# A fused attention and gated projection kernel on Trainium2: the output projection's eight tiles of a chunk issued in one run at the chunk's end instead of two runs of four, and one exponential moved ahead of a sigmoid

## The chip, the cores and the metric

One Trainium2 chip, all 8 cores, one program on each; every core computes one batch element. The metric is the device time in microseconds of the slowest core. Each core runs its engines (PE matmul, DVE vector, ACT scalar, POOL and SP, which here issue DMAs) from instruction streams of their own, joined by semaphores.

## What is computed

Per batch element there are 2048 tokens of width 4096. The reference, cut to what matters:

```python
xn = layernorm(x)
q, k, v = xn @ Wq, xn @ Wk, xn @ Wv            # 32 q heads, 8 k/v heads of 128
o_lin = gla_scan(softmax(q), softmax(k), v, log_sigmoid(k) / 16)   # recurrent state S per head
y = sliding_window_attn(rope(q), rope(k), v)    # window 64
s = bf16(0.5 * y + 0.5 * o_lin) @ Wo            # output projection
g = silu(xn @ W0.T + b0 + masked low-rank terms)
out = x + s * g
```

## The kernel before, in words

The work runs in stages. Stage 1 normalises x and transposes it into `bigA`. Stage 2 computes g (4096 base matmuls, line 210) and spills it to `g_sp` in HBM. Stage 3 computes v, k and q (lines 272, 299, 326) and spills them. Then the attention goes over 16 chunks of 128 tokens, `for c in range(NCH)` at line 464, and the output projection, called p5 in the code, is woven into it.

A chunk has three parts. The **k part** loads `kin` (line 467), takes sigmoid and log of it on ACT (lines 474 and 476), scans it on DVE (line 478), takes exponentials (482, 485, 490), and `ek`, the exponential of `kin` (line 492), whose column sums are two PE matmuls `denk` (495, 496); ACT turns them into reciprocals `rk` (499 to 502). The **q part** goes over 8 groups of four q heads: `eq` (555), `denq` (558), `p4rq` (562, 563), rotary products (569, 577 to 583). The **score part** goes over the same 8 groups: scores (602 to 614), exponentials (620, 624), sums (628, 631), reciprocals (638, 639), products (642, 646), the linear term (650, 655), and, two groups later, `emit_pass2` with the output matmuls (417 to 422), the copy into `bigA` (435), the state update (442, 452, 459). In this program chunks c=0 to 3 are attention alone; from c=4 on each chunk also carries 8 tiles of the projection for the 512 tokens finished four chunks and more ago; 32 tiles for the last 512 tokens follow after c=15.

A **p5 tile** is emitted by `emit_p5_jtile` (line 358). It is 32 matmuls into the one PSUM tile `pWo` (line 381), a copy by ACT, `scop` (390), a multiply with g on DVE, `sg` (393), a DMA transpose issued from ACT's queue, `sgt` (397), an add of x on DVE, `xadd` (402), and the store of the result from SP's queue, `outst` (406). The tile's g comes by `gld` from SP's queue (367), its x by `xld` from POOL's queue (371). Two tiles share one block of Wo, 2 MB in HBM, loaded from POOL's queue by `emit_p5_block` (352) into one of two buffers, so that four tiles can have their weights in SBUF at once. A matmul group of a tile waits for the copy of the tile before.

Every queue takes its instructions in the order of the program, and a wait holds all that is behind it. On SP's queue the order is gld of tile n, outst of tile n, gld of tile n+1; outst of n waits for xadd of n, so gld of n+1 is not issued before xadd of n. On POOL's queue a Wo block stands behind the xld of the tile before it, and that xld waits for the xadd two tiles back. On DVE, sg and xadd of a tile stand ahead of whatever the program has next, and on ACT the transpose of a tile stands ahead of what is next there.

Of the 8 tiles of a chunk, before, four stand between the q part and the score part, and four after the score part, ahead of two small copies on DVE, `sbf` (668) and `p4odone` (670); the next chunk's `vin` load (470) waits for `p4odone`. SP's queue has nothing of the score part in it, nor has POOL's.

Of the kernel before, what the change touches and what calls it, by code (L numbers as in the profile page):

```python
# [9 lines left out]
AF = mybir.ActivationFunctionType  # L10
# [22 lines left out]
class Walk:  # L33
# [26 lines left out]
    def op(self, stream, name, emit_fn, waits=()):  # L60
        serial = stream in ("V", "S", "G")
        sem = STREAM_SEM[stream]
        if self.mode == "collect":
            self._wait(waits)
            return
        if self.mode == "count":
            if serial:
                self.C[sem] += 1
                if name is not None:
                    self.evt[name] = (sem, self.C[sem])  # L70
            elif name is not None and name in self.waited:
                self.C[sem] += 1
                self.evt[name] = (sem, self.C[sem])
            return
        if self.stream != stream:
            return
        self._wait(waits)
        if serial and self.C[sem] > 0:
            self.eng.wait_ge(self.sems[sem], self.C[sem])
        instr = emit_fn(self.eng)  # L80
        if serial:
            self.C[sem] += 1
            instr.then_inc(self.sems[sem], 1)
        elif name is not None and name in self.waited:
            self.C[sem] += 1
            instr.then_inc(self.sems[sem], 1)
# [34 lines left out]
def build_walk(w, t):  # L121
    op, dma = w.op, w.dma
# [9 lines left out]
    for i in range(NTT):  # L132
# [5 lines left out]
            waits=[f"p1xn.{i-2}"] if i >= 2 else [])  # L138
# [3 lines left out]
           waits=[f"p1x.{i}"] + ([f"p1r.{i-2}"] if i >= 2 else []))  # L142
# [3 lines left out]
           waits=[f"p1x.{i}"] + ([f"p1xn.{i-2}"] if i >= 2 else []))  # L146
# [6 lines left out]
           waits=[f"p1sq.{i}"])  # L153
# [4 lines left out]
           waits=[f"p1r.{i}", f"p1nm.{i}"] + ([f"p1tr.{i-2}"] if i >= 2 else []))  # L158
# [4 lines left out]
            waits=[f"p1xn.{i}"])  # L163
# [5 lines left out]
        waits=P1_END)  # L169
    dma("G", "w_bt", lambda e: e.dma_start(out=t["bt"], in_=t["bt_h"][:]), waits=P1_END)  # L170
    xn = t["bigA"][:].rearrange("p (k tt) -> p k tt", k=32)
    for ts in range(4):
        def mm_h(e, ts=ts):
# [6 lines left out]
           waits=["w_acat", f"p1tr.{NTT-1}"] + ([f"p2hev.{ts-1}"] if ts else []))  # L180
        op("S", f"p2hev.{ts}",
           lambda e, ts=ts: e.copy(t["h"][:, ts * 512:(ts + 1) * 512], pb[0][:]),
           waits=[f"p2h.{ts}"])
# [9 lines left out]
    for lt in range(128):  # L193
        j, ts = lt // 4, lt % 4
# [4 lines left out]
            waits=P1_END if lt < 2 else [f"p2tl3.{lt - 2}"])  # L199
# [60 lines left out]
    for vq in range(4):  # L260
# [4 lines left out]
            waits=[f"p2mm.{119 + 8 * vq}"] if vq < 2 else [f"p3vmm.{(vq-1)*16 - 1}"])  # L265
        for tt in range(16):
            it = vq * 16 + tt

            def mm_v(e, vq=vq, tt=tt, it=it):
# [6 lines left out]
               waits=[f"wv.{vq}"] + ([f"p3vev.{it-2}"] if it >= 2 else [f"p2sil.{126}", f"p2sil.{127}"]))  # L276
            op("S", f"p3vev.{it}",
               lambda e, it=it: e.copy(t["ev"][it % 4][:, 0:256], pb[4 + it % 2][:, 0:256]),
               waits=[f"p3vmm.{it}"] + ([f"p3vsp.{it-4}"] if it >= 4 else P2_POOL_FREE),)
# [4 lines left out]
                waits=[f"p3vev.{it}"])  # L284
    for b in range(4):
# [4 lines left out]
            waits=[f"p3vmm.{47 + 16 * b}"] if b < 2 else [f"p3kmm.{(b-1)*8 - 1}"])  # L290
        for sub in range(8):
            j2, ts = sub // 4, sub % 4
            j = b * 2 + j2
            it = b * 8 + sub

            def mm_k(e, b=b, j2=j2, ts=ts, it=it):
# [7 lines left out]
               waits=[f"wk.{b}"] + ([f"p3kev.{it-2}"] if it >= 2 else [f"p3vev.{62 + it}"]))  # L304
            op("S", f"p3kev.{it}",
               lambda e, it=it: e.copy(t["ev"][it % 4], pb[4 + it % 2][:]),
               waits=[f"p3kmm.{it}"] + ([f"p3ksp.{it-4}"] if it >= 4 else [f"p3vsp.{60 + it}"]))
# [4 lines left out]
                waits=[f"p3kev.{it}"])  # L312
    for b in range(16):
# [3 lines left out]
            waits=[f"p3kmm.{23 + 8 * b}"] if b < 2 else [f"p3qmm.{(b-1)*8 - 1}"])  # L317
        for sub in range(8):
            j2, ts = sub // 4, sub % 4
            j = b * 2 + j2  # L320
            it = b * 8 + sub

            def mm_q(e, b=b, j2=j2, ts=ts, it=it):
# [7 lines left out]
               waits=[f"wqb.{b}"] + ([f"p3qev.{it-2}"] if it >= 2 else [f"p3kev.{30 + it}"]))  # L331
            op("S", f"p3qev.{it}",
               lambda e, it=it: e.copy(t["ev"][it % 4], pb[4 + it % 2][:]),  # L333
               waits=[f"p3qmm.{it}"] + ([f"p3qsp.{it-4}"] if it >= 4 else [f"p3ksp.{28 + it}"]))
# [4 lines left out]
                waits=[f"p3qev.{it}"])  # L339
# [5 lines left out]
       waits=P3_SPILLED + [f"p3qev.{127}"])  # L345
# [11 lines left out]
    def emit_p5_jtile(ts, j):  # L357
        b, j2 = j // 2, j % 2
        it = j * 4 + ts
        if j2 == 0:  # L360
            emit_p5_block(ts, b)
        ei = len(p5_seq)
        prev = p5_seq[-1] if p5_seq else None
        pprev = p5_seq[-2] if len(p5_seq) >= 2 else None
        p5_seq.append(it)
        dma("SY", f"gld.{it}",
            lambda e, j=j, ts=ts, ei=ei: e.dma_start(
                out=t["gld5"][ei % 2], in_=t["g_sp"][j, :, ts * 512:(ts + 1) * 512]),
            waits=[f"p2gs.{it}"] + ([f"sg.{pprev}"] if pprev is not None else []))
        dma("G", f"xld.{it}",  # L370
            lambda e, j=j, ts=ts, ei=ei: e.dma_start(  # L371
                out=t["xld5"][ei % 2],
                in_=bass.AP(t["x_h"].tensor, ts * 512 * D + j * 128,
                            [[D, 128], [128 * D, 4], [1, 128]])),
            waits=[f"xadd.{pprev}"] if pprev is not None else [])

        def mm_s(e, b=b, j2=j2, ts=ts):
            wb = t["wobuf"][b % 2].rearrange("p (k m) -> p k m", k=32)
            off = (4 * ts % 8) * 128
            for k in range(32):  # L380
                ii = e.matmul(t["pWo"][:], wb[:, k, j2 * 128:j2 * 128 + 128],  # L381
                              bass.AP(t["bigA"][:].tensor, k * 1024 + off,
                                      [[32 * NT, 128], [1, 512]]),
                              start=(k == 0), stop=(k == 31))
            return ii
        op("T", f"p5mm.{it}", mm_s,
           waits=[f"wo.{ts}.{b}", f"oev.{4*ts+3}.{KVH-1}"] +
                 ([f"scop.{prev}"] if prev is not None else []))
        op("S", f"scop.{it}",
           lambda e, ei=ei: e.copy(t["sgf5"][ei % 2], t["pWo"][:]),  # L390
           waits=[f"p5mm.{it}"] + ([f"sg.{pprev}", f"outst.{pprev}"] if pprev is not None else []))
        op("V", f"sg.{it}",
           lambda e, it=it, ei=ei: e.tensor_tensor(t["sgv5"][ei % 2], t["sgf5"][ei % 2],  # L393
                                                   t["gld5"][ei % 2], ALU.mult),
           waits=[f"scop.{it}", f"gld.{it}"] + ([f"sgt.{pprev}"] if pprev is not None else []))
        dma("S", f"sgt.{it}",
            lambda e, it=it, ei=ei: e.dma_start_transpose(
                t["sgt5"][ei % 2].rearrange("p (r q) -> p r q", r=4),
                t["sgv5"][ei % 2]),
            waits=[f"sg.{it}"] + ([f"xadd.{pprev}"] if pprev is not None else []))  # L400
        op("V", f"xadd.{it}",
           lambda e, ei=ei: e.tensor_tensor(t["sgf5"][ei % 2].bitcast(BF16).bitcast(F32),  # L402
                                            t["xld5"][ei % 2], t["sgt5"][ei % 2], ALU.add),
           waits=[f"sgt.{it}", f"xld.{it}"] + ([f"outst.{pprev}"] if pprev is not None else []))
        dma("SY", f"outst.{it}",
            lambda e, j=j, ts=ts, ei=ei: e.dma_start(
                out=bass.AP(t["out_h"].tensor, ts * 512 * D + j * 128,
                            [[D, 128], [128 * D, 4], [1, 128]]),
                in_=t["sgf5"][ei % 2].bitcast(BF16).bitcast(F32)),
            waits=[f"xadd.{it}"])  # L410
# [53 lines left out]
    for c in range(NCH):  # L464
        cr = c % 2
        dma("SY", f"kin.{c}",
            lambda e, c=c: e.dma_start(out=t["kin"], in_=t["k_sp"][c, :, :]),
            waits=P3_SPILLED + ([f"p4kdone.{c-1}"] if c else []))
        dma("SY", f"vin.{c}",
            lambda e, c=c, cr=cr: e.dma_start(out=t["vring"][cr], in_=t["v_sp"][c, :, :]),  # L470
            waits=(P3_SPILLED + ["s_zero"] if c < 2 else []) +
                  ([f"p4odone.{c-1}"] if c >= 1 else []) +
                  ([f"sadd.{c-2}.{KVH-1}"] if c >= 2 else []))
        op("S", f"sig.{c}", lambda e: e.activation(t["ksig"], t["kin"], AF.Sigmoid),
           waits=[f"kin.{c}"])
        op("S", f"lsig.{c}", lambda e: e.activation(t["ksig"], t["ksig"], AF.Ln), waits=[])  # L476
# [4 lines left out]
           waits=[f"lsig.{c}", "c_onesf"])  # L481
# [7 lines left out]
           waits=[f"lam.{c}"] + ([f"sdec.{c-1}.{KVH-1}"] if c else []))  # L489
        op("S", f"expli.{c}", lambda e: e.activation(t["expli"], t["lam"], AF.Exp, scale=-INV16),  # L490
           waits=[f"lam.{c}"])
        op("S", f"ek.{c}", lambda e: e.activation(t["ekt"], t["kin"], AF.Exp),  # L492
           waits=[f"kin.{c}"])
        op("T", f"denk.{c}",
           lambda e: (e.matmul(pb[4][:], t["ones_sb"][:], t["ekt"][:, 0:512], start=True, stop=True),  # L495
                      e.matmul(pb[5][:], t["ones_sb"][:], t["ekt"][:, 512:1024], start=True, stop=True))[-1],
# [86 lines left out]
                   lambda e, g=g: e.tensor_tensor(t["sqa8"][g], t["sq2"], t["sq3"], ALU.add)],  # L583
               waits=[f"rotq.{c}.{g}"])

        if c >= 4:
            _ts = (c - 4) // 4
            _j0 = 8 * ((c - 4) % 4)
            for _j in range(_j0, _j0 + 4):
                emit_p5_jtile(_ts, _j)  # L590
        for g in range(KVH):
            gr = g % 2
            hs = slice(g * 128, (g + 1) * 128)
# [66 lines left out]
                emit_pass2(c, g - 2, cr)  # L660
        emit_pass2(c, KVH - 2, cr)
        emit_pass2(c, KVH - 1, cr)
        if c >= 4:
            _ts = (c - 4) // 4
            _j0 = 8 * ((c - 4) % 4)
            for _j in range(_j0 + 4, _j0 + 8):
                emit_p5_jtile(_ts, _j)
        op("V", f"sbf.{c}", lambda e: e.tensor_copy(t["Sbf"], t["S"]),
           waits=[f"sadd.{c}.{KVH-1}"])
        op("V", f"p4odone.{c}", lambda e: e.tensor_copy(t["qt2"][:, 0:1], t["qtil3"][0][:, 0:1]),  # L670
           waits=[f"oev.{c}.{KVH-1}", f"oev.{c}.{KVH-2}"])

    for j in range(32):
        emit_p5_jtile(3, j)
    P4_END = [f"p4odone.{NCH-1}", f"sadd.{NCH-1}.{KVH-1}", f"sbf.{NCH-1}",
# [267 lines left out]
```

## Time and profile before

| | |
|---|---|
| median of 2 runs | 6549.73 us |
| lowest and highest | 6541.64 and 6557.82 us |
| the profiled execution's own time | 6541.64 us |
| its span (slowest core, core 4) | 6540.1 us |
| spans of the 8 cores | 6479.1 to 6540.1 us |
| busy: PE, DVE, ACT, POOL | 4181.4, 1384.1, 1244.0, 372.7 us |

The profile is of the slowest core. Busy times are summed over the whole span and say little on a single stage, since the stages have different limits. The chunks c=4 to 14 take 2239 us of the span, and c=15 with the last 32 tiles about 640.

### The profile page before, as it was taken

Reading aid. Unit: us, or ns where it says so; the run is one execution under the profiler, and the core shown is the slowest. Engines: PE = TensorE matmul, PEld = TensorE weight load, DVE = VectorE, ACT = ScalarE, POOL = GpSimd, SP = SyncE. Lnnn points to the kernel's source line nnn. Section 1 sums busy time; section 2 is a strip of 40 time slices with the busy share of each in tenths; the row PEclk is TensorE's granted clock in tenths of the full one; section 3 lists DMA queues with packets and bytes.
Section 4 is the critical chain, followed back from the end, with each engine's and each line's share of the span. In section 5 each row is a group of like instructions: output and inputs, shape, how many; then the busy total and the mean of one; then the engine's idle time right before and its main releaser. Section 6 shows DMA issues by size and latency. Waiting matters only on the chain.

```text
span 6540.1 us, 54373 instructions; the slowest of 8 cores (6479.1 to 6540.1 us)
## 1 busy us (share of the span) xinstructions
PE 4181.4 (64%) x18464; PEld 1753.7 (27%) x18464; DVE 1384.1 (21%) x2344; ACT 1244.0 (19%) x1790; POOL 372.7 (6%) x368
## 2 busy tenths in 40 slices
PE   0047777787799999999844545545456444564555
PEld 0012332232258444444310112211122111121222
DVE  2212222222220000000044332322322323223111
ACT  4420000000001000000144332222322223223000
POOL 0000000000000000000000000000000000000111
PEclk9998988898899999999955667767677676776888
DMA  5454334434443333333310246364554544544898
GB/s 144 137 100 92 85 91 93 93 80 94 90 88 58 58 58 58 58 58 58 57 23 17 37 82 100 61 100 79 86 100 72 90 89 75 100 78 84 120 148 136
DMA packets 821746, 544.02 MB, mean 83 GB/s; under 512 B 241248, under 2 KB 757600, under 8 KB 819296
## 3 DMA queue, kind: packets, MB, share of 16 engines
q0 software_dynamic: 460576, 320.89, 32.1%
q1 hardware_dynamic: 225216, 186.09, 10.9%
q10 hardware_dynamic: 135680, 33.57, 3.2%
q8 instruction: 150, 2.46, 0.2%
q14 instruction: 124, 1.02, 0.1%
HBM read 634.83 MB, written 92.27 MB: 111 GB/s over the span
## 4 chain that ended last, share of the span: by engine, by line
PE 46%; DMA 24%; ACT 12%; DVE 9%; issue 5%; ACTq 3%; SPq 1%; DVEq 1%; POOLq 0%; POOL 0%
PE pb L326 14%; PE pb L210 13%; DMA bigA<-bigA 9%; DMA bigA<-g_sp 8%; DMA pool<-maskt 4%; PE pb L272 3%; PE pb L299 3%; PE pWo L381 3%; ACTq L160 2%; PE pb L239 2%; DMA pool<-q_sp 2%; DVE bigA L393 1%; DVE bigA L402 1%; ACT pool L245 1%; ACT pool L140 1%
## 5 line engine op out<-in xcount | busy, mean ns | idle before, releaser
L381 PE MATMUL pWo<-bigA 128*128 128x512 bf16 x4096 | 960.7, 395 | 258.3 <-DMA bigA<-wo 176.6
L210 PE MATMUL pb<-bigA,pool 128*128 128x512 bf16 x4096 | 935.3, 388 | 134.2 <-ACT pool L245 133.3
L326 PE MATMUL pb<-bigA,pool 128*128 128x512 bf16 x4096 | 884.2, 379 | 0.0
L381 PEld LDWEIGHTS pWo<-bigA 128*128 128x128 bf16 x4096 | 407.4, 101 | 806.4 <-issue 384.2
L227 DVE TENSOR_TENSOR pool<-pb,pool 128x512 bf16<-128x512 f32 x512 | 354.2, 692 | 1180.8 <-PE pb L239 695.8
L210 PEld LDWEIGHTS pb<-bigA,pool 128*128 128x128 bf16 x4096 | 399.0, 99 | 676.0 <-issue 240.0
L326 PEld LDWEIGHTS pb<-bigA,pool 128*128 128x128 bf16 x4096 | 400.8, 98 | 483.3
L478 DVE TENSOR_TENSOR_SCAN pool<-onesf_sb,pool 128x128 f32<-128x128 f32 x128 | 54.4, 425 | 1455.5 <-ACT pool L476 1444.0
L245 ACT ACTIVATE pool<-pb,b_sb 128x512 f32<-128x512 f32 x128 | 87.9, 687 | 1366.2 <-PE pb L239 1366.2
L558 PE MATMUL pb<-pool,twos_sb 128*128 128x512 bf16 x128 | 74.9, 585 | 381.5 <-ACT pool L555 381.5
L495 PE MATMUL pb<-pool,ones_sb 128*128 128x512 bf16 x16 | 9.3, 584 | 456.2 <-ACT pool L492 456.2
L176 PE MATMUL pb<-bigA,pool 128*128 128x512 bf16 x128 | 30.6, 400 | 409.5 <-DMA pool<-acat 406.8
L390 ACT COPY bigA<-pWo 128x512 f32<-128x512 f32 x128 | 74.9, 585 | 1125.3 <-PE pWo L381 1054.6
L628 PE MATMUL pb<-pool,twos_sb 128*128 128x512 bf16 x128 | 63.7, 498 | 326.3 <-ACT pool L624 317.0
L371 POOL DMA_DIRECT2D bigA<-x x128 | 96.6, 755 | 3065.0 <-DVE bigA L402 2930.4
L393 DVE TENSOR_TENSOR bigA<-bigA 128x512 bf16<-128x512 f32 x128 | 88.6, 692 | 739.2 <-DMA bigA<-g_sp 602.0
L333 ACT CAST pool<-pb 128x512 bf16<-128x512 f32 x128 | 74.9, 585 | 809.2 <-PE pb L326 809.2
L272 PE MATMUL pb<-pool,bigA 128*128 128x256 bf16 x2048 | 225.9, 274 | 1.0 <-ACT pool L245 1.0
L299 PE MATMUL pb<-bigA,pool 128*128 128x512 bf16 x1024 | 221.2, 379 | 0.0
L402 DVE TENSOR_TENSOR bigA<-bigA 128x512 f32<-128x512 f32 x128 | 88.6, 692 | 617.9 <-DMA bigA<-bigA 617.9
L272 PEld LDWEIGHTS pb<-pool,bigA 128*128 128x128 bf16 x2048 | 201.3, 98 | 26.2 <-issue 1.9
L219 PE MATMUL pb<-pool 16*128 16x512 bf16 x512 | 53.6, 408 | 215.9 <-DVE pool L227 215.9
(112 smaller groups left out, 3423.2 us busy)
## 6 DMA issues: line engine op xcount, KB each, us to landing
bigA<-wo POOLq DMA_DIRECT2D x64, 2048.0 KB, 17.4
pool<-maskt POOLq DMA_DIRECT2D x128, 512.0 KB, 4.6
pool<-x SPq DMA_DIRECT2D x16, 2048.0 KB, 8.3
pool<-w0t POOLq DMA_DIRECT2D x16, 2048.0 KB, 18.1
g_sp<-pool SPq DMA_DIRECT2D x128, 256.0 KB, 2.7
pool<-wq POOLq DMA_DIRECT2D x16, 2048.0 KB, 17.2
bigA<-x POOLq DMA_DIRECT2D x128, 256.0 KB, 5.2
bigA<-g_sp SPq DMA_DIRECT2D x128, 256.0 KB, 4.5
```

What stands on the lines that cost most here:

```text
L160: lambda e, i=i, ib=ib: e.dma_start_transpose(t["bigA"][:].rearrange("p (c tt) -> p c tt", c=32)[:, :, i * 128:(i + 1) * 128], t["xn_tm"][ ...
L210: ii = e.matmul(pb[bk][:], wb[:, k, j2 * 128:j2 * 128 + 128], xn[:, k, ts * 512:(ts + 1) * 512], start=(k == 0), stop=False)
L227: lambda e, l=l, ts=ts, it=it: e.tensor_tensor(t["tl"][l], pb[l][:], t["mbig"][it % 2].rearrange("p (l4 tt) -> p l4 tt", l4=4)[:, l, :], A ...
L239: ii = e.matmul(pb[bk][:], t["id128_sb"][:], t["tl"][l], start=False, stop=(l == 3))
L245: lambda e, it=it, j=j, bk=bk: e.activation(t["gv"][it % 2], pb[bk][:], AF.Silu, bias=t["b0_sb"][:, j:j + 1]),
L272: ii = e.matmul(pb[4 + it % 2][:, 0:256], xn[:, k, tt * 128:(tt + 1) * 128], wb[:, k, :], start=(k == 0), stop=(k == 31))
L299: ii = e.matmul(pb[4 + it % 2][:], wb[:, k, j2 * 128:j2 * 128 + 128], xn[:, k, ts * 512:(ts + 1) * 512], start=(k == 0), stop=(k == 31))
L326: ii = e.matmul(pb[4 + it % 2][:], wb[:, k, j2 * 128:j2 * 128 + 128], xn[:, k, ts * 512:(ts + 1) * 512], start=(k == 0), stop=(k == 31))
L371: lambda e, j=j, ts=ts, ei=ei: e.dma_start(out=t["xld5"][ei % 2], in_=bass.AP(t["x_h"].tensor, ts * 512 * D + j * 128, [[D, 128], [128 * D ...
L381: ii = e.matmul(t["pWo"][:], wb[:, k, j2 * 128:j2 * 128 + 128], bass.AP(t["bigA"][:].tensor, k * 1024 + off, [[32 * NT, 128], [1, 512]]), ...
L393: lambda e, it=it, ei=ei: e.tensor_tensor(t["sgv5"][ei % 2], t["sgf5"][ei % 2], t["gld5"][ei % 2], ALU.mult),
L402: lambda e, ei=ei: e.tensor_tensor(t["sgf5"][ei % 2].bitcast(BF16).bitcast(F32), t["xld5"][ei % 2], t["sgt5"][ei % 2], ALU.add),
```

## The change

Two edits. The p5 tiles of a chunk are emitted in one run of eight, after the score part and after `sbf` and `p4odone`, and no longer in two runs of four. And `ek` is emitted as the first ACT operation of the k part, ahead of the sigmoid, with one more wait, for `sk` of the chunk before on DVE, which reads the buffer that `ek` writes.

```diff
@@ -471,6 +471,8 @@
+        op("S", f"ek.{c}", lambda e: e.activation(t["ekt"], t["kin"], AF.Exp),
+           waits=[f"kin.{c}"] + ([f"sk.{c-1}"] if c else []))
         op("S", f"sig.{c}", lambda e: e.activation(t["ksig"], t["kin"], AF.Sigmoid),
            waits=[f"kin.{c}"])
@@ -489,8 +491,6 @@
-        op("S", f"ek.{c}", lambda e: e.activation(t["ekt"], t["kin"], AF.Exp),
-           waits=[f"kin.{c}"])
         op("T", f"denk.{c}",
@@ -583,11 +583,6 @@
-        if c >= 4:
-            _ts = (c - 4) // 4
-            _j0 = 8 * ((c - 4) % 4)
-            for _j in range(_j0, _j0 + 4):
-                emit_p5_jtile(_ts, _j)
         for g in range(KVH):
@@ -660,16 +655,15 @@
-        if c >= 4:
-            _ts = (c - 4) // 4
-            _j0 = 8 * ((c - 4) % 4)
-            for _j in range(_j0 + 4, _j0 + 8):
-                emit_p5_jtile(_ts, _j)
         op("V", f"sbf.{c}", lambda e: e.tensor_copy(t["Sbf"], t["S"]),
            waits=[f"sadd.{c}.{KVH-1}"])
         op("V", f"p4odone.{c}", lambda e: e.tensor_copy(t["qt2"][:, 0:1], t["qtil3"][0][:, 0:1]),
            waits=[f"oev.{c}.{KVH-1}", f"oev.{c}.{KVH-2}"])
-
+        if c >= 4:
+            ts = (c - 4) // 4
+            j0 = 8 * ((c - 4) % 4)
+            for j in range(j0, j0 + 8):
+                emit_p5_jtile(ts, j)
```

On PE, in chunk c=4 of the kernel before, the first four tiles (128 matmuls, L381) stand between the last rotary matmul of the q part (L569) and the first scores (L602):

```order
L558 MATMUL pb<-pool,twos_sb 128x512
L569 MATMUL pb<-pool,rmat_sb 128x512
L381 MATMUL pWo<-bigA 128x512 x128
L602 MATMUL pb<-bigA,pool 128x512
L603 MATMUL pb<-i4rep_sb,mcur_sb 128x512
```

On PE in the same chunk of the changed kernel the scores (its L597 is the L602 of before) follow the q part directly:

```order
L569 MATMUL pb<-pool,rmat_sb 128x512
L558 MATMUL pb<-pool,twos_sb 128x512
L569 MATMUL pb<-pool,rmat_sb 128x512
L597 MATMUL pb<-bigA,pool 128x512
L598 MATMUL pb<-i4rep_sb,mcur_sb 128x512
```

The four tiles have left this place. At the chunk's end of the changed kernel all 256 matmuls of the eight tiles stand in a row, between the last state matmul (L442) and the next chunk's denk (L495):

```order
L422 MATMUL pb<-pool 128x512
L442 MATMUL pS<-pool 128x128
L381 MATMUL pWo<-bigA 128x512 x256
L495 MATMUL pb<-pool,ones_sb 128x512
L496 MATMUL pb<-pool,ones_sb 128x512
```

On ACT in the k part of chunk c=4, before: sigmoid (L474), log (L476), the three exponentials of the scan (L482, L485, L490), ek (L492), then the first operation on denk's result (L499):

```order
L474 ACTIVATE pool<-pool 128x1024
L476 ACTIVATE pool<-pool 128x1024
L482 ACTIVATE pool<-pool 128x1024
L485 ACTIVATE st<-pool 128x8
L490 ACTIVATE pool<-pool 128x1024
L492 ACTIVATE pool<-pool 128x1024
L499 ACTIVATE pool<-pb 128x512
```

On ACT in the changed kernel, where L474 is ek, L476 the sigmoid, L478 the log and L484, L487, L492 the three exponentials of the scan:

```order
L474 ACTIVATE pool<-pool 128x1024
L476 ACTIVATE pool<-pool 128x1024
L478 ACTIVATE pool<-pool 128x1024
L484 ACTIVATE pool<-pool 128x1024
L487 ACTIVATE st<-pool 128x8
L492 ACTIVATE pool<-pool 128x1024
L499 ACTIVATE pool<-pb 128x512
```

Nothing now stands on ACT between the last scan exponential and L499. On SP's and POOL's queues the order of the DMAs is the same in both kernels.

## Rows read from the trace of the kernel before

**Rows 1.** Page, section 2: 40 slices of 163.5 us each.

```profile
PE   0047777787799999999844545545456444564555
PEclk9998988898899999999955667767677676776888
DMA  5454334434443333333310246364554544544898
```

**Rows 2.** Timeline of ACT: k parts of chunks 4 and 15 begin (start us, us).

```profile
3661.82 1.06 ACT L474 ACTIVATE pool<-pool 128x1024 f32<-128x1024 bf16 x1
...
5900.99 1.06 ACT L474 ACTIVATE pool<-pool 128x1024 f32<-128x1024 bf16 x1
```

**Rows 3.** Windows: chunk 11 by stage (length, busy and count by engine, PEclk, DMA, GB/s).

```profile
5088.30:5143.60 55.30, 10.92 (x29) 2.86 (x30) 22.24 (x43) 23.93 (x35) 0.00 (x0) 0.50 0.40 63
5143.60:5195.00 51.40, 30.98 (x135) 13.04 (x133) 7.94 (x14) 4.68 (x8) 3.98 (x4) 0.83 0.62 97
5195.00:5238.60 43.60, 32.53 (x92) 7.74 (x92) 21.25 (x41) 19.74 (x34) 2.44 (x2) 0.73 0.45 67
5238.60:5286.50 47.90, 29.62 (x129) 12.55 (x128) 6.88 (x10) 3.95 (x8) 3.95 (x4) 0.86 0.59 104
5286.50:5291.50 5.00, 0.00 (x0) 0.00 (x0) 0.88 (x3) 1.29 (x2) 2.44 (x2) 0.50 0.72 219
```

**Rows 4.** Windows: chunk 3, which has no tiles; its score part.

```profile
3607.40:3658.40 51.00, 41.08 (x97) 8.99 (x96) 23.71 (x46) 21.91 (x38) 0.00 (x0) 0.58 0.00 1
```

**Rows 5.** Chain that ended last, core 4, from the fifth tile of chunk 15 on.

```profile
6073.73 0.70 DVE bigA L402
6075.04 5.10 DMA bigA<-g_sp
6080.30 0.70 DVE bigA L393
6081.12 11.61 DMA bigA<-bigA
6093.03 0.70 DVE bigA L402
```

**Rows 6.** Timeline, PE and POOL, core 4: the run from chunk 15's fifth tile on.

```profile
6052.94 7.07 PE L381 MATMUL pWo<-bigA 128*128 128x512 bf16 x32
...
6075.78 1.71 POOL L352 DMA_DIRECT2D bigA<-wo  x1
...
6101.80 8.60 PE L381 MATMUL pWo<-bigA 128*128 128x512 bf16 x32 [17.80 <-DMA bigA<-wo]
```

**Rows 7.** Timeline of DVE, core 4: xadd of the run's eighth and 32nd tile.

```profile
6168.40 0.69 DVE L402 TENSOR_TENSOR bigA<-bigA 128x512 f32<-128x512 f32 x1 [2.88 <-DMA bigA<-bigA]
...
6492.92 0.69 DVE L402 TENSOR_TENSOR bigA<-bigA 128x512 f32<-128x512 f32 x1 [3.24 <-DMA bigA<-bigA]
```

**Rows 8.** Timeline of core 7: the same run's first tile and eighth xadd.

```profile
5978.41 7.07 PE L381 MATMUL pWo<-bigA 128*128 128x512 bf16 x32
...
6082.90 0.69 DVE L402 TENSOR_TENSOR bigA<-bigA 128x512 f32<-128x512 f32 x1 [2.89 <-DMA bigA<-bigA]
```

**Rows 9.** Timeline of core 1: the same two.

```profile
6030.25 7.07 PE L381 MATMUL pWo<-bigA 128*128 128x512 bf16 x32
...
6153.20 0.69 DVE L402 TENSOR_TENSOR bigA<-bigA 128x512 f32<-128x512 f32 x1 [2.91 <-DMA bigA<-bigA]
```

**Rows 10.** Timeline of ACT: the k part of chunk 12.

```profile
5290.20 1.28 ACT L474 ACT_TABLE_LOAD   x1 [18.39 <-DMA pool<-k_sp]
...
5292.62 1.28 ACT L476 ACT_TABLE_LOAD   x1
...
5299.41 1.06 ACT L482 ACTIVATE pool<-pool 128x1024 bf16<-128x1024 f32 x1 [4.44 <-DVE pool L478]
...
5302.02 1.06 ACT L492 ACTIVATE pool<-pool 128x1024 bf16<-128x1024 bf16 x1
5304.38 0.60 ACT L499 ACTIVATE pool<-pb 128x512 f32<-128x512 f32 x1 [1.31 <-PE pb L496]
```

## The prediction

> **What bounds the kernel now.** I read the 40 slices of the page first, then the starts of the chunks, then the stages of one chunk, and last the chain of waits through the projection's tiles.
>
> The slices [rows 1] show two kinds of time. In the first half PE is busy seven to nine tenths; from about 3300 us on it is busy four to six tenths, at a granted clock of 0.6 to 0.7. The change touches that second part alone. Its size comes from the starts of the k parts [rows 2]: chunks 4 to 14 take 5900.99 - 3661.82 = 2239.2 us, or 203.6 us each, eleven times. Chunk 11 is close to that mean, and the windows cut it at the borders of its parts [rows 3]: 55.3 us for the k and q parts, 51.4 for the first run of four tiles (first matmul to last xadd on DVE), 43.6 for what is left of the score part, 47.9 for the second run, and 5.0 until the next chunk's first ACT operation, together 203.2.
>
> In no part is one engine full. In a run of four PE is busy 30 of 48 to 51 us [rows 3]. The chain shows why [rows 5]: it goes from an xadd on DVE to the next g (gld, 5.1 us), the multiply sg (0.7), the DMA transpose (11.6) and the next xadd, in a ring, with no matmul in it. By the order of SP's queue gld of a tile is not issued before xadd of the tile before, so the ring is serial. A tile on PE takes 7.07 us, and the next starts 8.0 after it; the ring took 6093.03 - 6073.73 = 19.3 us that time, with a Wo load of 2 MB issued at 6075.78 in flight [rows 5, 6]. So a run of tiles is paced by DMAs and DVE's place in the ring, and PE runs ahead until the weights are missing.
>
> **Part 1, the two runs become one.** Removed from the middle of the chunk: a run that occupies 51.4 us. But the score part then no longer finds its head start. Before, PE had issued the first scores while DVE was still at its xadds, and found a warmer clock (0.73). Without tiles ahead of it the same score part took 51.0 us in chunk 3, at 0.58 [rows 4]. I take 50.0; the bounds are 43.6 and 51.0. The gld, xld and transposes of those four tiles leave too, and go where the matmuls go.
>
> Added at the end: a run of eight in place of one of four, 47.9 us before. What does it take? The trace has it: in chunk 15 the second run of four goes straight on into the 32 last tiles, so 36 stand in a row, with the same two buffers for Wo, and the first four tiles' weights already there, as they will be in the changed kernel. From the run's first matmul to the end of its eighth xadd it took
>
> - core 4: 6168.40 + 0.69 - 6052.94 = 116.2 us [rows 6, 7]
> - core 7: 6082.90 + 0.69 - 5978.41 = 105.2 us [rows 8], the shortest of the eight cores
> - core 1: 6153.20 + 0.69 - 6030.25 = 123.6 us [rows 9], the longest; the middle of the eight is about 109.
>
> It is not twice 47.9 = 95.8, since only four tiles have their weights beforehand. The Wo block of tiles 5 and 6 is issued on POOL's queue behind an xld that waits for the second tile's xadd: 6075.78, 22.8 us into the run, and tile 5 starts at 6101.80 after PE stood 17.8 us for it [rows 6]. The next two blocks follow in the same way and slow the transposes of the tiles whose ring they cross. Before, of a chunk's four blocks two landed beside the k, q or score part, where nothing waited for them: by the order of POOL's queue one was issued behind the last xld of each run. Afterwards it is one of four. Further on in the long run a pair of tiles costs (6492.92 - 6168.40) / 12 = 27.0 us [rows 7], which would make 47.9 + 2 x 27.0 = 102.0 for eight. I take 108: between 102.0 and core 4's own 116.2, near the middle of the eight cores. The bounds are 95.8 and 123.6.
>
> On the last wait: `p4odone` now stands ahead of the tiles, so that `vin` is free earlier. I cost it at nothing, because SP's queue keeps `kin` and `vin` behind the eighth outst in any case, which waits for the eighth xadd. The 5.0 us from there to the sigmoid stay [rows 3]. Nor does the first part of the chunk gain from the move: POOL and SP issue in the same order as before.
>
> **Part 2, ek moved.** Before, from ek's start to the start of the reciprocals on ACT 5304.38 - 5302.02 = 2.36 us pass: ek itself, and a wait of 1.31 for PE [rows 10]. Now denk is done under the sigmoid and the scan, and these 2.36 go. At the front ek costs its 1.06 and the step to the next, 1.1 together, since sigmoid, log and DVE's scan follow one on another. Net -1.2 us per chunk; bounds -2.4 (if the front were hidden) and +0.1 (if a table load of 1.28 were added each time). The added wait on sk of the chunk before is met in the k part of that chunk, a whole q and score part earlier, and holds nothing behind it.
>
> No table load should be added past the first chunk: L482's exponential runs after L476's log without one [rows 10], so both are in one table, and that is the one resident when the next chunk's ek comes, since only copies, scalings, exponentials and logs lie between. In chunk 0 one is added, +1.3.
>
> The Trainium skill, page "ScalarE: Activation LUTs", section "Table sets: the hidden batching unit", asks for calls to be grouped by table, and putting an exponential ahead of a sigmoid looks like the opposite. The same page ("What ACT_TABLE_LOAD costs") gives 2.66 us for a switch with its drain, 43 us over 16 chunks if each had one more; the trace has 1.28 us for a load, and the next operation on its heels, which would make 21.
>
> **The sum.** A chunk from 4 to 14: 55.3 - 1.2 + 50.0 + 108 + 5.0 = 217.1, against 203.6: +13.5, times 11 = +148.5. Chunk 15 and the end: before, its long run starts 6052.94 - 5900.99 = 152.0 us after its sigmoid; afterwards at 55.3 - 1.2 + 50.0 = 104.1, 47.9 earlier, but with four tiles more in it, 2 x 27.0 = 54.0: +6.1. Chunks 0 to 3: 4 x -1.2 + 1.3 = -3.5. Together +151. The profiled execution's own time was 6541.64 (span 6540.1), 8 us under the median of 6549.73; against the median the forecast is 6549.7 + 151 = 6701 us, 2.3% slower. About 2%, 131 us, is what a measurement of this kernel can tell from no change.
>
> **The rivals.**
>
> *Paced by PE (faster).* If the second four tiles came at PE's own step of 8.0 us, a run of eight would be 47.9 + 32 = 79.9, a chunk 189.0, and the whole 11 x -14.6 + 2.6 = -158: 6392 us. It decides from the point where ring and weights of a tile take under 8.0 us. For it: one start-up and one tail fewer per chunk, and a run holds the clock at 0.83 to 0.86, where the parts around it have 0.50 and 0.73 [rows 3]. Against it: eight of eight cores took 105 us or more.
> The Trainium skill says it as a rule: page "Perfetto Trace Analysis", section "Matmul Optimizations", asks that matmuls execute back to back in batches, because the engine scales with its use. By that rule the time would be this rival's. The fifth tile, which takes 8.60 us after its wait and not 7.07 [rows 6], speaks against it: the longer batch has the wait inside.
>
> *The second four cost a run of their own (no change).* With 95.8 for eight and 51.0 for the score part a chunk takes 205.9, +2.3, and with the other terms (+3.6) the whole +29: 6579 us. With the 102.0 of the long run's pace and 50.0 it is 211.1, +7.5, together +85: 6635. For it: in chunk 15 all cores come to load Wo without a pause, in the middle of the kernel a core does so half of the time. Against it: core 7, with little in its way, still took 105.2.
>
> *Contention as in core 4 or worse (slower still).* With 116.2 the whole is +151 + 11 x 8.2 = +241: 6791 us; with core 1's 123.6 it is 6872. For it: the measured time is that of the slowest core, and this one is core 4 here. Against it: it would have to be so in every chunk.
>
> *The change does not do what it says.* The ek edit could be lost behind DVE's scan: 15 to 20 us at most, within the range.
>
> **How the numbers follow.** A run of eight near 108 (104 to 114): 0.55, of which most lies over +131. Cheaper runs, no change: 0.27. Contention at 114 or more: 0.13. Paced by PE: 0.05. Slower by over 2% is then 0.48 + 0.13 = 0.61, within 2% 0.07 + 0.27 = 0.34, faster 0.05. The range is 6600 to 6795: the lower end is between the two figures of the no-change rival, the upper one core 4's run in every chunk.
>
> **What would show it.** The starts of the k parts 215 to 219 us apart in chunks 5 to 14. In each run of eight two waits of PE for a DMA into bigA from wo, 8 to 18 us each, at its fifth and seventh tile; 104 to 114 us from first matmul to eighth xadd. The score part at 47 to 51 us with a granted clock near 0.6. In the k part one table load ahead of the sigmoid and one ahead of the log, and no wait of ACT for L496. A spacing under 200 us would prove the forecast wrong, and a run of eight under 100 us would name the step.

## The result, and the profile after

The change makes the kernel slower, by less than 2% but beyond doubt: ratio to the kernel before 1.0139, 95% interval 1.0123 to 1.0155. Its executions take 6634.7 to 6647.0 us, against 6541.0 to 6557.8 before; by the ratio it is 91 us more than the 6549.7. The profiled execution took 6638.9 us. (Either kernel has executions in which one die runs at a lower clock, some 260 to 420 us longer; ratios and times leave these out, and where an experiment's profile shows such a die, its means below are of the four cores at the usual clock, which are named.)

The page of the changed kernel, sections 1 and 2 in part, and the tile group of section 5 (busy and mean, idle before, releaser), then the same group of the kernel before:

```profile
span 6637.3 us, 54375 instructions; the slowest of 8 cores (6569.7 to 6637.3 us)
PE 4258.5 (64%) x18464; PEld 1763.2 (27%) x18464; DVE 1384.0 (21%) x2344; ACT 1245.9 (19%) x1791; POOL 372.6 (6%) x368
...
DMA  5454434443443333333200247633674446633998
...
L381 PE MATMUL pWo<-bigA 128*128 128x512 bf16 x4096 | 994.5, 405 | 537.7 <-DMA bigA<-wo 467.1
```

```profile
L381 PE MATMUL pWo<-bigA 128*128 128x512 bf16 x4096 | 960.7, 395 | 258.3 <-DMA bigA<-wo 176.6
```

PE's time ahead of the tiles' matmuls rose to 537.7 us, 467.1 of it on loads of Wo. The kernel before had 258.3 and 176.6. The DMA digits of the chunks now swing between 3 and 7, where [rows 1] had mostly 4 and 5.

The stages of chunk 11 on core 5, the slowest here: k and q parts, score part, run of eight, and what follows to the next chunk (columns as in [rows 3]):

```profile
5165.20:5218.20 53.00, 11.10 (x28) 2.72 (x28) 22.33 (x44) 25.39 (x36) 0.00 (x0) 0.50 0.40 72
5218.20:5265.70 47.50, 36.83 (x97) 8.44 (x97) 23.58 (x45) 21.92 (x38) 0.00 (x0) 0.66 0.00 1
5265.70:5368.80 103.10, 60.56 (x258) 25.43 (x257) 13.27 (x20) 6.29 (x12) 10.38 (x10) 0.84 0.80 125
5368.80:5372.50 3.70, 0.00 (x0) 0.00 (x0) 0.04 (x1) 0.00 (x0) 2.44 (x2) 0.50 0.69 170
```

During the score part the DMA engines now do nothing (share 0.00), and during the run they are 0.80 busy; before, both runs and the score part between them had 0.45 to 0.62 [rows 3].

Mean over the eight cores and chunks 4 to 14, in us:

| | before | after |
|---|---|---|
| from the k part's first operation to the end of the q part | 55.5 | 54.0 |
| first run of four | 48.7 | none |
| score part, or what is left of it after that run | 44.4 | 49.0 |
| last run (four, or eight) | 48.6 | 103.8 |
| to the next chunk's first operation | 5.3 | 4.4 |
| chunk | 202.2 | 211.2 |

The column of before adds up to 0.3 too much, mostly because the run's first matmul starts 0.2 before the last rotary product ends. So the eight tiles themselves cost 103.8 - 97.3 = 6.5 more and the score part 4.6 more; 1.5 come back in the k and q parts and 0.9 in the step to the next chunk: +9.0 a chunk, 99 us in 11 chunks.

The run of eight of chunk 11, core 5: xadd of the second to the last tile (DVE), the Wo loads (POOL) and the two matmul groups that wait (PE), from the timelines of these engines:

```profile
5286.83 0.69 DVE L402 TENSOR_TENSOR bigA<-bigA 128x512 f32<-128x512 f32 x1 [2.92 <-DMA bigA<-bigA]
5305.70 0.69 DVE L402 TENSOR_TENSOR bigA<-bigA 128x512 f32<-128x512 f32 x1 [9.20 <-DMA bigA<-bigA]
5315.22 0.69 DVE L402 TENSOR_TENSOR bigA<-bigA 128x512 f32<-128x512 f32 x1 [2.90 <-DMA bigA<-bigA]
5334.93 0.69 DVE L402 TENSOR_TENSOR bigA<-bigA 128x512 f32<-128x512 f32 x1 [8.67 <-DMA bigA<-bigA]
5343.97 0.69 DVE L402 TENSOR_TENSOR bigA<-bigA 128x512 f32<-128x512 f32 x1 [2.90 <-DMA bigA<-bigA]
5358.12 0.69 DVE L402 TENSOR_TENSOR bigA<-bigA 128x512 f32<-128x512 f32 x1 [8.18 <-DMA bigA<-bigA]
5368.14 0.69 DVE L402 TENSOR_TENSOR bigA<-bigA 128x512 f32<-128x512 f32 x1 [2.91 <-DMA bigA<-bigA]
...
5288.88 1.72 POOL L352 DMA_DIRECT2D bigA<-wo  x1
5317.34 1.69 POOL L352 DMA_DIRECT2D bigA<-wo  x1
5346.01 1.71 POOL L352 DMA_DIRECT2D bigA<-wo  x1
...
5310.40 9.37 PE L381 MATMUL pWo<-bigA 128*128 128x512 bf16 x32 [13.71 <-DMA bigA<-wo]
5338.95 8.75 PE L381 MATMUL pWo<-bigA 128*128 128x512 bf16 x32 [11.18 <-DMA bigA<-wo]
```

The spacing of the xadds alternates: 18.9, 9.5, 19.7, 9.0, 14.2, 10.0. The wait in brackets alternates with it: a transpose lands 2.9 us after DVE's last work when no load is in flight, and 8.2 to 9.2 us after it when a load of Wo was issued some 2 us after the xadd before. I call such a step of the ring a turn.

The kernel before has one such long turn in each run of four, the third. Here are the second and third xadd and the load that was issued between them, in the second run of chunk 10, core 5:

```profile
5012.20 0.69 DVE L402 TENSOR_TENSOR bigA<-bigA 128x512 f32<-128x512 f32 x1 [2.92 <-DMA bigA<-bigA]
5026.56 0.69 DVE L402 TENSOR_TENSOR bigA<-bigA 128x512 f32<-128x512 f32 x1 [8.29 <-DMA bigA<-bigA]
...
5014.25 1.71 POOL L352 DMA_DIRECT2D bigA<-wo  x1
```

Over all cores of the changed kernel, 408 of the tiles' 1024 transposes had a load of Wo of their own core in flight at some time between issue and landing: they took 8.4 us (median). The other 616 took 2.5. In the last 32 tiles, where every core has a load of Wo in flight about two thirds of the time, none of the 120 with a load of their own core beside them took under 7.2 us, and none of the 136 without one over 3.3. So it is the core's own load that counts, and not those of the other cores.

The k part of chunk 12, ACT, core 5:

```profile
5372.55 1.06 ACT L474 ACTIVATE pool<-pool 128x1024 bf16<-128x1024 bf16 x1 [16.05 <-DMA pool<-k_sp]
5373.68 1.28 ACT L476 ACT_TABLE_LOAD   x1
...
5376.10 1.28 ACT L478 ACT_TABLE_LOAD   x1
...
5384.35 1.06 ACT L492 ACTIVATE pool<-pool 128x1024 bf16<-128x1024 f32 x1
5385.49 0.60 ACT L499 ACTIVATE pool<-pb 128x512 f32<-128x512 f32 x1
```

ek (L474) runs without a table load, two loads follow as before, and L499 comes on the heels of L492, where [rows 10] had ek and a wait of 1.31 between.

### The profile page after: what moved, and what is told of

It is laid out like the page before. It is cut to its first block, busy times and chain, and to the rows that moved or that the text cites. A ratio compares the mean times of both kernels' runs of the same rounds, so it can differ in the third digit from the quotient of the medians.

```text
span 6637.3 us, 54375 instructions; the slowest of 8 cores (6569.7 to 6637.3 us)
## 1 busy us (share of the span) xinstructions
PE 4258.5 (64%) x18464; PEld 1763.2 (27%) x18464; DVE 1384.0 (21%) x2344; ACT 1245.9 (19%) x1791; POOL 372.6 (6%) x368
## 3 DMA queue, kind: packets, MB, share of 16 engines
q1 hardware_dynamic: 225216, 186.09, 10.6%
## 4 chain that ended last, share of the span: by engine, by line
PE 45%; DMA 25%; ACT 12%; DVE 9%; issue 5%; ACTq 3%; SPq 1%; DVEq 1%; POOLq 0%; POOL 0%
PE pb L326 13%; PE pb L210 13%; DMA bigA<-bigA 9%; DMA bigA<-g_sp 9%; DMA pool<-maskt 4%; PE pb L272 3%; PE pb L299 3%; ACTq L160 2%; PE pb L239 2%; PE pWo L381 2%; DMA pool<-q_sp 1%; DVE bigA L393 1%; DVE bigA L402 1%; ACT pool L245 1%; ACT pool L619 1%
## 5 line engine op out<-in xcount | busy, mean ns | idle before, releaser
L381 PE MATMUL pWo<-bigA 128*128 128x512 bf16 x4096 | 994.5, 405 | 537.7 <-DMA bigA<-wo 467.1
L381 PEld LDWEIGHTS pWo<-bigA 128*128 128x128 bf16 x4096 | 413.2, 103 | 1113.8 <-issue 712.1
L495 PE MATMUL pb<-pool,ones_sb 128*128 128x512 bf16 x16 | 9.4, 585 | 243.1 <-ACT pool L474 243.1
```

## The experiments

I went in with two theories for the length of a run. R: it is a serial ring of gld, sg, transpose and xadd, and a Wo load in flight stretches a turn. W: it is PE's wait for weights inside the run, most of the 467 us of the page.

**The two edits apart.** `e1_run8_only` is the changed kernel with ek at its old place:

```diff
-        op("S", f"ek.{c}", ...)                 # ahead of sig.{c}
+        op("S", f"ek.{c}", ...)                 # after expli.{c}, as before
```

> The eight tiles in one run at the chunk's end, ek left where it was. Theory R (a run is paced by the serial ring gld, sg, transpose, xadd, and a Wo load in flight makes every second turn of it long): a run of eight stays at 101 to 107 us, the chunk is 1.0 to 1.3 us longer than in the changed kernel, 211.2 + 1.2 = 212.4 us, and the whole is 15 to 20 us over the changed kernel, 1.016 to 1.018 of before. Rival (ek ahead of the sigmoid delays the scan and costs time): the whole is under the changed kernel, below 1.0139.

Measured: 1.0217 of before, interval 1.0093 to 1.0341. The interval is too wide to part the two expectations; the trace does it. On cores 4 to 7 the chunk is 212.2 us and the run of eight 103.9. The chunk is 1.4 longer than on the same cores of the changed kernel (210.8), and that is the step from the last xadd to the next chunk's first operation, 5.8 us for 4.3. All the loss sits in the order of the tiles.

`e2_ek_only` is the kernel before with ek moved:

> The kernel before with ek moved ahead of the sigmoid and nothing else. If the step saves 1.2 us in each of 16 chunks and costs one table load of 1.3 in the first: 18 us less, 0.997 of before, and no wait of ACT for denk's second matmul. If the front of the k part were hidden too: 2.4 us a chunk, 0.994. If it costs: over 1.000.

Measured: 0.9952, interval 0.9908 to 0.9995. The chunk falls from 202.2 to 200.9, 1.3 us, as the first expectation has it, and the step from the last xadd to the next chunk's first operation from 5.3 to 3.9 (18 us, 0.997, is inside the interval; 0.994 cannot be excluded by the ratio, but a chunk shorter by 2.4 would be at 199.8). The edit is a small gain.

**Ring or weights.** `e7_run8_wo_ahead` issues each load one tile earlier:

```diff
-        if j2 == 0:
-            emit_p5_block(ts, b)
+        if ei == 0:
+            emit_p5_block(ts, b)
...
+        if j2 == 1 and ei < 127:
+            emit_p5_block(ts if b < 15 else ts + 1, (b + 1) % 16)
         dma("G", f"xld.{it}",
```

> The changed kernel with each Wo block issued on POOL one tile earlier, ahead of the xld of the odd tile before it. Theory R: PE's two waits in a run fall from about 12 us each to 2 to 5, but the ring goes on as before, a run of eight 100 to 106 us, the whole within 30 us of the changed kernel. Theory W: each of the two waits falls by about 8 us and the run with them, to 88 us; chunks at 195, the whole about 200 us under the changed kernel.

Measured: 1.0226, interval 1.0097 to 1.0355; chunk 219.7, run of eight 112.4. Both theories missed: W by sign, since the waits for weights are gone (see the tile group of the page below, where PE's idle time is put down to ACT's copy) and the run is 8.6 us longer; R by size.

```profile
L383 PE MATMUL pWo<-bigA 128*128 128x512 bf16 x4015 | 997.3, 408 | 475.8 <-ACT bigA L392 470.8
```

The timelines of chunk 11, core 5, show what I had not thought of (xadds of the first, second, third, seventh and eighth tile, then the loads, then the fifth tile's matmuls):

```profile
5306.56 0.69 DVE L404 TENSOR_TENSOR bigA<-bigA 128x512 f32<-128x512 f32 x1 [3.35 <-DMA bigA<-bigA]
5320.63 0.69 DVE L404 TENSOR_TENSOR bigA<-bigA 128x512 f32<-128x512 f32 x1 [8.15 <-DMA bigA<-bigA]
5332.39 0.69 DVE L404 TENSOR_TENSOR bigA<-bigA 128x512 f32<-128x512 f32 x1 [2.93 <-DMA bigA<-bigA]
...
5387.47 0.69 DVE L404 TENSOR_TENSOR bigA<-bigA 128x512 f32<-128x512 f32 x1 [2.93 <-DMA bigA<-bigA]
5403.02 0.69 DVE L404 TENSOR_TENSOR bigA<-bigA 128x512 f32<-128x512 f32 x1 [8.64 <-DMA bigA<-bigA]
...
5310.35 1.70 POOL L352 DMA_DIRECT2D bigA<-wo  x1 [1.73 <-PE pWo L383]
5334.44 1.71 POOL L352 DMA_DIRECT2D bigA<-wo  x1
5363.71 1.69 POOL L352 DMA_DIRECT2D bigA<-wo  x1
5389.52 1.72 POOL L352 DMA_DIRECT2D bigA<-wo  x1
...
5331.72 8.78 PE L383 MATMUL pWo<-bigA 128*128 128x512 bf16 x32 [6.29 <-ACT bigA L392]
```

The fifth tile now waits for ACT's copy, and so for the ring. The long turns are the second, fourth, sixth and eighth: the fourth load, which in the changed kernel was issued after the eighth xadd, now falls into the run. That gave theory C: a turn is about 10 us alone and 16 with a load in flight, and what counts is how many loads cross a run (cross means: are in flight during it).

`e5_run8_gld_ahead` opens the ring at gld:

```diff
+        if ei + 1 < 128:
+            emit_gld(ei + 1)      # gld of the next tile, ahead of
         dma("SY", f"outst.{it}",  # this tile's store
```

> The changed kernel with gld of tile n+1 issued on SP ahead of outst of tile n, so that the ring is broken at gld; the Wo loads stay as they are. Theory R (the ring is the pace): short turns go from 9 to 8 us (PE's step), long ones from 19 to 13 or so, a run of eight from 104 to 84 to 92 us, chunks from 211 to 193 to 199, the whole 200 to 330 us under the changed kernel. Theory W (the pace is the Wo loads, for which PE waits at the fifth and seventh tile): a run of eight stays at 98 to 104 and the whole within 60 us of the changed kernel.

Measured: 6529.6 us in a single execution, too few for a ratio; the chunk on cores 4 to 7 is 204.4, the run of eight 97.2, where these cores had 210.8 and 102.9. That lies between the two expectations, and both missed: R by size, with 5.7 us of the 12 to 20, and W because the run is just under its 98 to 104 and a chunk 6.4 shorter, 70 us in 11. Three rows of core 5, chunk 11 (the fourth and fifth xadd and the fifth tile's matmuls), show why:

```profile
5212.78 0.69 DVE L412 TENSOR_TENSOR bigA<-bigA 128x512 f32<-128x512 f32 x1 [8.22 <-DMA bigA<-bigA]
5230.00 0.69 DVE L412 TENSOR_TENSOR bigA<-bigA 128x512 f32<-128x512 f32 x1 [9.55 <-DMA bigA<-bigA]
...
5209.96 8.78 PE L391 MATMUL pWo<-bigA 128*128 128x512 bf16 x32 [9.37 <-DMA bigA<-wo]
```

With the ring open it meets the loads at once: the transposes take 8 to 9 us also in turns that were short, and the fifth tile's turn starts from its late weights. In the means of these cores the waits for the transpose are 8.7 to 9.6 us in five of the eight turns. Both limits lie close together; neither theory alone was the whole.

**Taking the loads away.** `e3_run8_no_wo` and `e4_run4_no_wo` leave out all Wo loads but the first two, in the changed kernel and in the one before:

```diff
+        if ts == 0 and b < 2:
             dma("G", f"wo.{ts}.{b}", ...)
...
-           waits=[f"wo.{ts}.{b}", ...
+           waits=[f"wo.0.{b % 2}", ...
```

> The changed kernel without the Wo loads after the first two blocks (the tiles then use wrong weights; 124 MB of loads are left out). Theory C (a run is a serial ring of about 9 us a tile, and what makes it longer is each Wo load that is in flight during it): a run of eight falls from 104 to 13 + 7 x 9.1 = 77 us or a little under, the last 32 tiles from 27 to 18 us a pair, PE waits for ACT or DVE only. Rival P (with the weights there, PE's own step of 8.0 us is the pace): 8.0 us a tile, 70 us a run and 16.0 us a pair.

> The kernel before without the Wo loads after the first two blocks (wrong weights for the tiles, the loads left out). Theory C: a run of four falls from 48.6 to 13 + 3 x 9.1 = 40 us; two runs of four then take 80 and one of eight 77, so that the two orders of the tiles come to within 1% of each other in the whole, the chunk of this kernel at 184 to 188 us. Rival (two short runs lose more than one long one in start and end, loads apart): this kernel is over 2% slower than the changed one without its loads.

Measured: 6220.9 us with runs of eight, 6197.4 with runs of four, 0.4% apart, from one execution each. The spans of the eight cores have the same mean, 6171.5 and 6172.1. Chunks take 184.0 and 185.6, and 1.3 of the 1.6 between them is what ek is worth, which only the first of the two kernels has moved; a run of eight 78.6, the two runs of four 41.7 and 40.7; the last tiles 19.2 and 18.9 us a pair. C holds, 1.6 us over its 77 for a run of eight, and P, the pace of PE, is out: with the weights there from the start, a tile still takes over 9 us. The run of eight of core 5, chunk 11, last four xadds and the last matmul group:

```profile
5258.19 0.69 DVE L403 TENSOR_TENSOR bigA<-bigA 128x512 f32<-128x512 f32 x1 [2.90 <-DMA bigA<-bigA]
5267.23 0.69 DVE L403 TENSOR_TENSOR bigA<-bigA 128x512 f32<-128x512 f32 x1 [2.90 <-DMA bigA<-bigA]
5276.32 0.69 DVE L403 TENSOR_TENSOR bigA<-bigA 128x512 f32<-128x512 f32 x1 [2.92 <-DMA bigA<-bigA]
5285.63 0.69 DVE L403 TENSOR_TENSOR bigA<-bigA 128x512 f32<-128x512 f32 x1 [2.91 <-DMA bigA<-bigA]
...
5266.60 7.07 PE L382 MATMUL pWo<-bigA 128*128 128x512 bf16 x32 [1.99 <-ACT bigA L391]
```

Turns of 9.0, 9.1 and 9.3, every transpose 2.9 us after, and PE held by ACT's copy, which waits for the ring.

**One load out of the run.** `e9_run8_late_load` takes the third load out of the changed kernel's run, `e10_run4_late_load` the only one out of each run of four of the kernel before:

```diff
+        late = 2 <= ei // 2 < 48 and ei // 2 % 2 == 0   # e9: 4 <= ..., % 4 == 0
-        if j2 == 0:
+        if j2 == 0 and not late:
             emit_p5_block(ts, b)
...                                # gld and xld of the tile
+        if j2 == 1 and late:
+            emit_p5_block(ts, b)
```

> The changed kernel with one load moved: the first Wo block of the next chunk is issued after the eighth xadd of a run and no longer after the sixth, so that two loads and not three are in flight during a run of eight, and both of the next chunk's lie beside its k part. Theory C: the run falls by 8 to 10 us to 94 to 96, the chunk from 211 to 201 to 204, the whole about 100 us under the changed kernel, that is equal to the kernel before. Rival W (the pace is PE's wait for weights inside the run, which this leaves as it is): run and whole within 30 us of the changed kernel.

Measured: 1.0011, interval 0.9951 to 1.0071: level with the kernel before, as C has it. On cores 0 to 3 the run is 98.0 us and the chunk 204.8, where the same cores of the changed kernel have 104.7 and 211.6; that is 2 us and 1 us over the expectation. PE's wait for weights stayed, so W is out a second time (tile group of the page, core 5):

```profile
L384 PE MATMUL pWo<-bigA 128*128 128x512 bf16 x4096 | 987.6, 403 | 503.4 <-DMA bigA<-wo 433.7
```

> The kernel before with the load that was issued in the middle of each run of four issued after the run's fourth xadd, together with the one that stood there already. Theory C: no load is in flight during a run, a run of four falls from 48.6 to 39 to 41 us, a chunk from 202 to 184 to 188, the whole 170 to 220 us under the kernel before, 0.967 to 0.974 of it. Rival (two loads issued together, 4 MB, do not land before the next run 44 us later, or slow the q part's loads): PE waits for Wo at a run's first or third tile, and the whole is within 60 us of the kernel before.

Measured: 0.9749, interval 0.9648 to 0.9851, so faster than both kernels. The run of four is 43.3 and the chunk 191.1. The direction is C's, the size is not: I had 39 to 41 and 184 to 188. The second turn of a run takes 10.7 in place of 9.3, and it is the load of g that is slower: from the first xadd to the second multiply 6.3 us pass, where the kernel without loads has 5.0. Both Wo loads have landed by then; why g is late, no run of mine shows.

The turns side by side, means over the cores and runs of chunks 4 to 14 (us; the first is from the run's first matmul to the first xadd's end; the late load in a run of eight on cores 0 to 3):

| kernel | turns | loads that cross the run |
|---|---|---|
| before | 13.7, 9.9, 15.0, 10.0 | 1 |
| late load, runs of four | 13.6, 10.7, 9.6, 9.3 | 0 |
| no loads, runs of four | 13.6, 9.3, 9.2, 9.2 | 0 |
| after | 12.8, 9.7, 16.2, 10.6, 16.9, 10.8, 16.4, 10.6 | 3 |
| late load, run of eight | 12.9, 9.6, 16.1, 10.9, 16.8, 10.3, 10.4, 10.9 | 2 |
| loads one tile ahead | 12.8, 15.7, 11.9, 16.9, 10.8, 17.3, 10.7, 16.4 | 4 |
| no loads, run of eight | 12.7, 9.2, 9.3, 9.4, 9.4, 9.6, 9.6, 9.5 | 0 |

Each load makes one turn long, by 5 to 6 us over the short turns beside it, and which one follows from where it is issued. Its whole price is higher, since the short turns beside it are slower too than those without any load. The three loads of a run of eight cost 103.8 - 78.6 = 25.2 us, 8.4 each; the two of a chunk's two runs of four cost 97.3 - 82.4 = 14.9, 7.5 each. And with no load at all, one run of eight is 82.4 - 78.6 = 3.8 us cheaper than two of four. So the 6.5 that the tiles lost are 10.3 for the loads less 3.8 for the start that is saved.

**Hiding the ring.** `e11_run4_late_ek` adds the ek edit to the late load:

> The kernel with two runs of four and no load in flight in them, and ek ahead of the sigmoid too. The two savings add, since one lies in the runs and the other in the k part: chunks at 189.5 to 190.2 (191.1 less 1.3), the whole 15 to 20 us under that kernel, 0.971 to 0.973 of before. If ek's step were hidden by the loads that now lie beside the k part, chunks stay at 191.

Measured: 0.9734, interval 0.9632 to 0.9835; chunk 189.6, 1.5 under that of the late load alone. In the chunk they add; the two ratios are too close to tell apart.

`e8_woven` gives up runs. One tile goes into each of the eight groups of the score part:

```diff
+            if p5n is not None:
+                p5_mm(p5n)        # matmuls and copy, ahead of the sums dsw
             def mm_dsw(...)
...
+                p5_sg(p5n)        # xadd, store of the tile before; sg; next gld, xld, Wo
             op("V", f"pcn.{c}.{g}", ...)
...
+                p5_tr(p5n)        # the transpose
             op("T", f"at.{c}.{g}", ...)
```

> One tile in each of the 8 groups of the score part, its matmuls between the scores and the sums, its copy after the exponentials, sg and the transpose before the group's products, and its xadd and store only with the next tile, so that DVE never stands at a fresh transpose; gld and xld of the next tile are issued behind sg. Theory C (in a run of tiles PE and the attention wait for a ring of DMAs; the ring's latency is hidden when attention lies between its steps): a group takes 11 to 13 us in place of 6.3 for the attention and 12 to 13 for the tile, the score part with its 8 tiles 90 to 105 us, a chunk 150 to 165, the whole 5950 to 6150 us. Rival (the Wo loads, one every two groups, take as long here as in the last tiles, 26 to 27 us a pair of tiles): a group takes over 13 us, the score part 110 or more, a chunk 170 or more, the whole 6200 or more.

Measured: 0.8952, interval 0.8824 to 0.908, times of 5864 to 5925 us, under the range I gave. Two starts of k parts on core 4, ACT, and section 2 of the page in part:

```profile
4741.88 1.06 ACT L507 ACTIVATE pool<-pool 128x1024 f32<-128x1024 bf16 x1
...
4894.16 1.06 ACT L507 ACTIVATE pool<-pool 128x1024 f32<-128x1024 bf16 x1
```

```profile
DMA  5463434344444343343341300877777777777999
```

That chunk of core 4 is 152.3 us; the mean over cores and chunks is 151.6, from 202.2, and inside the expectation. The whole came out under it because the last 32 tiles, which I had left as they were, gained as well: chunk 15 and the end went from 639.1 to 523.6 us. The DMA digits are 7 all through the chunks, no longer 3 and then 7: the same transfers, spread. The loads still stretch the ring, 909 of the 1024 transposes have one beside them and take 8.4 us, but attention stands between its steps.

This kernel changes several things at once: the places of the tiles, the load of g ahead of the store, the xadd one tile late, the places of the loads. No run takes them apart. Of the 50.6 us of a chunk, the nearest single edits were worth 11.1 (loads out of the runs of four) and 5.7 (g ahead, in a run of eight); that the rest is the weaving is argued, not shown.

## Why the prediction was right in direction and too large

The forecast was 6701 us, +151; it came to +91, inside the range of 6600 to 6795, but in the case to which I had given 0.34 (within 2%) and not in that with 0.61.

- *The run of eight.* Taken at 108, bounds 95.8 and 123.6; measured 103.8. This is the term that was mis-sized: 4.2 us, 46 in 11 chunks. I read it from eight tiles of chunk 15, which took 111.6 in the mean of the cores; core 4's 116.2 and core 1's 123.6 occur in none of the changed kernel's 88 runs of eight in chunks 4 to 14, the longest of which is 115.3, and the means of its cores lie between 99.3 and 108.0. Why those eight tiles were slower is not shown: the first eight of chunk 15 in the changed kernel took 102.0, though there too all cores come to load without a pause. The figure from the pace of the long run, 102.0, would have been nearer. The mechanism was in the text: three loads cross the runs of a chunk where two did, they slow the transposes, and PE waits at the fifth and seventh tile (13.71 and 11.18 us). The waits are the sign of a load and not its price; the price is the ring's, 10.3 us more for the loads, less 3.8 for the start that is saved. That saving stood only among the reasons of a rival.
- *The score part.* 50.0 against 49.0, at a granted clock of 0.66 in the windows above where 0.58 was expected from chunk 3.
- *The q part* I left as it was. From k part start to q part end it is 54.0 where it was 55.5; with no loads it is 53.3 and 53.7. That took off some 16 us in all, which I had put at nothing; no run of mine explains it.
- *ek.* -1.2 forecast; -1.3 in the kernel before alone. Within the changed kernel the k part is as long as before (22.0 us to its last copy on DVE), and the step from the last xadd to its first operation is 4.4, where it is 5.3 before and 5.8 in the changed kernel without this edit. The one table load in chunk 0 is there: 1791 ACT instructions for 1790.
- *Chunk 15 and the end.* +6.1 forecast; its length went from 639.1 to 636.3 in the mean of the cores, -2.8.
- *The sum.* +13.5 a chunk forecast, +9.0 measured: 49 us; with 9 for the end, nearly all of the 60 that are missing.
- *The signs.* The k parts lie 211.2 us apart, under the 215 to 219 that I named, and the run of eight, at 103.8, is just under its 104 to 114; the two waits for Wo, the score part, the table loads and the missing wait for L496 are as named.
- *The rivals.* Paced by PE fell: a turn takes 9.2 to 9.6 us even without any load, and not 8.0. The Trainium skill's rule for it ("Perfetto Trace Analysis", "Matmul Optimizations": matmuls back to back, in batches) did not help here: the longer batch was granted a clock of 0.84, where the two runs of four had 0.83 and 0.86 [rows 3], PE was busy for 60.6 of its 103.1 us, and the kernel lost. The change-nothing rival, a second four at the price of a run of their own, has 95.8 for eight, 97.3 in the mean of the cores. Its second form, with 102.0 for the run and 50.0 for the score part, gave a chunk of 211.1 and 6635 us in all, against 211.2 and 6641 measured. I had it in hand and gave its side 0.27. That it comes so close is in part luck: its run is 1.8 short, and the score and q parts make up for it.

## What to carry to other kernels

Moving work into longer runs does not change how much of it there is, but it does change what else is in flight at the same time: count, for each stretch whose pace is a chain of small DMAs, the large loads that cross it, and issue those where only engines are busy (0.9749 of before, with nothing else changed). A long wait for weights in the profile can be covered entirely by a ring behind it; issuing each load earlier removed the wait here and made the kernel slower (1.0226), since one more load then crossed the run. The largest gain, 0.8952, came from the kernel that places independent work between the steps of the chain and reorders the chain's own loads as well; how much comes of which is not shown.

## What the runs showed of the hardware that I had not expected

A DMA transpose of 128 x 512 bf16 took 2.5 us from issue to landing when no load of Wo was in flight on its core, and 8.4 us beside one such load issued on another queue (medians of 616 and 408 in the changed kernel; 2.5 and 8.1 before; 2.5 for all 1024 without the loads). The load is of 4 MB: Wo is f32 in HBM, and the 2 MB named so far are what is written to SBUF as bf16. It landed 18.3 us after issue when it crossed a run and 17.1 when it did not (17.4 and 16.5 before). So the small transfer paid about three times its price, and the large one 5 to 7% more.

The loads of the other seven cores did not do this. Among the last 32 tiles, where all cores load most of the time, the transposes without a load of their own core beside them took 2.47 us (median of 136).
